# State decay product moved from GpSimd to ScalarE, and x added by an accumulating transfer

## What is computed

```
zxbcdt = xn @ in_proj_w.T            # z, x-B-C and dt per token
xBC    = silu(causal conv of 4 taps)
theta  = clip(theta_base + tanh(xn @ w1) @ w2, -pi/2, pi/2)
log_z  = complex(-(lambda + eta * theta**2) * dt, theta * dt)
# per chunk, with the running sum of log_z and the state of the chunk before:
S = exp(cumlog) * state + sum over s <= t of exp(cumlog_t - cumlog_s) B_s x_s
y = Re(C . S);  y = y + x_ssm * D
g = y * silu(z);  g = g * rsqrt(mean(g*g) + eps) * norm_w
mixer = g @ out_proj_w.T
expert = gate * (xn @ expert_w[idx] + expert_b[idx])
out = x + mixer + expert
```

## Time and profile before

| What | Value |
|---|---|
| median of three runs | 1242.69 us (1236.13 to 1245.13) |
| the profiled execution | 1231.05 us, its span 1229.2 us |
| TensorE matmul busy | 1063.8 us, 87% |
| VectorE busy | 1044.4 us, 85% |
| ScalarE busy | 815.0 us, 66% |
| GpSimd busy | 270.0 us, 22% |
| granted TensorE clock, mean | 0.942 |

### The profile page before, as it was taken

The page is one execution under the profiler, slowest core; times in us unless marked ns, Lnnn a source line. Parts: engine busy times, 40 slices in busy tenths (PEclk is TensorE's granted clock), DMA queues, the critical chain, the costliest instruction groups (busy, mean ns, idle before and its releaser), DMA issues.

```text
span 1229.2 us, 26224 instructions
## 1 busy us (share of the span) xinstructions
PE 1063.8 (87%) x8826; PEld 826.3 (67%) x8827; DVE 1044.4 (85%) x1934; ACT 815.0 (66%) x1453; POOL 270.0 (22%) x307
## 2 busy tenths in 40 slices
PE   3772299846899999999999999999999999999895
PEld 2441266544677777777777777777877777777674
DVE  5757923227999999999999999999999999999962
ACT  2441211108988888887888888888888888887650
POOL 1212676600011111221111111111122111111111
PEclk9895599977899999999999999999999999999997
DMA  6993155641444444444444444444444444444341
GB/s 231 360 363 122 35 163 178 168 119 45 146 145 149 144 153 143 148 136 150 152 148 144 144 151 152 144 153 144 144 136 146 154 145 150 145 148 144 125 138 33
DMA packets 144270, 185.55 MB, mean 151 GB/s; under 512 B 20142, under 2 KB 101343, under 8 KB 143760
## 3 DMA queue, kind: packets, MB, share of 16 engines
q1 hardware_dynamic: 122736, 146.70, 35.3%
q0 software_dynamic: 6528, 17.83, 5.6%
q10 hardware_dynamic: 14880, 19.40, 4.5%
HBM read 75.99 MB, written 40.63 MB: 95 GB/s over the span
## 4 chain that ended last, share of the span: by engine, by line
DVE 51%; issue 21%; PE 2%; POOL 1%; ACT 1%; DVEq 1%; DMA 0%; POOLq 0%; ACTq 0%
DVE conv L1143 13%; DVE att L1229 4%; DVE g L1247 3%; DVE prod L1202 3%; DVE decay L1176 3%; DVE prod L1201 3%; DVE prod L1212 3%; DVE prod L1211 3%; DVE o_tile L1269 2%; DVE phase L1168 2%; DVE x_tile L1254 2%; DVE lam L1160 2%; DVE state L1237 2%; DVE cown L1216 2%; DVE theta L1151 1%
## 5 line engine op out<-in xcount | busy, mean ns | idle before, releaser
L817 PE MATMUL ps<-xn_in,win 128*128 128x256 f32 x1152 | 289.5, 393 | 25.9 <-DMA xn_in<-xnT_d 15.6
L817 PEld LDWEIGHTS ps<-xn_in,win 128*128 128x128 f32 x1152 | 214.3, 195 | 57.3 <-issue 13.6
L1143 DVE SCALAR_TENSOR_TENSOR conv<-x_pre,col,conv 128x256 f32<-128x256 f32 x480 | 195.2, 479 | 15.6 <-ACT conv L984 15.5
L942 PE MATMUL ps<-wout,g 128*128 128x256 f32 x512 | 129.5, 398 | 23.8 <-DVE o_tile L1269 23.8
L1309 POOL TENSOR_TENSOR state_in<-state,cin_s 128x256 f32<-128x256 f32 x56 | 43.4, 775 | 478.3 <-DVE state L1237 478.3
L942 PEld LDWEIGHTS ps<-wout,g 128*128 128x128 f32 x512 | 97.9, 197 | 43.2 <-issue 29.4
L1322 POOL TENSOR_TENSOR rms<-ms,cst 128x1 f32<-128x1 f32 x64 | 46.6, 729 | 245.4 <-DVE ms L1261 245.4
L631 DVE TENSOR_TENSOR r_tiles<-ps,r_expw 128x256 f32<-128x256 f32 x72 | 30.6, 425 | 79.9 <-issue 73.7
L929 PEld LDWEIGHTS ps<-att,x_tok 128*64 128x64 f32 x1024 | 54.6, 136 | 49.6 <-issue 26.5
L984 ACT ACTIVATE conv<-ps,col 128x256 f32<-128x256 f32 x160 | 83.7, 572 | 0.0
L1229 DVE TENSOR_TENSOR att<-ps,cst 128x1024 f32<-128x1024 f32 x64 | 77.2, 1207 | 5.6 <-PE ps L902 5.6
(11 more groups left out here) (169 smaller groups left out, 2338.2 us busy)
## 6 DMA issues: line engine op xcount, KB each, us to landing
cin_s<-cin SPq DMA_DIRECT2D x128, 129.0 KB, 2.2
rep<-bc_d SPq DMA_DIRECT2D x128, 128.0 KB, 2.8
grow_s<-grow SPq DMA_DIRECT2D x128, 128.0 KB, 2.1
bup_s<-bup SPq DMA_DIRECT2D x128, 128.0 KB, 2.0
cown_s<-cown SPq DMA_DIRECT2D x128, 128.0 KB, 2.0
expert_d<-r_tiles ACTq DMA_DIRECT2D x18, 512.0 KB, 3.0
xn_d<-r_tokens SPq DMA_DIRECT2D x16, 512.0 KB, 9.1
xnT_d<-r_tiles ACTq DMA_DIRECT2D x16, 512.0 KB, 7.4
```

Of the source, the lines that this page charges most:

```text
L817: last = nc.tensor.matmul(dst, win[:, kt, n * P:(n + 1) * P], xn_in[b][:, kt, :], start=(kt == 0), stop=(kt == KT - 1))
L942: nc.tensor.matmul(bank_o[:, 0:D_MODEL], g[ch][:, q, :], wout[:, q, :], start=(q == 0), stop=(q == PAIRS - 1))
L1143: nc.vector.scalar_tensor_tensor(conv[:, ct, :], x_pre[b][:, ct, tap:tap + MT], c("conv_w", ct * D_CONV + tap), conv[:, ct, :], ALU.mult, ...
```

## The change

Four things are done together.

1. VectorE's `back_plus` is gone. The gathered expert rows land in `plus_tile` (two buffers per tile instead of one each of x and expert rows); ScalarE's new `back_scale` multiplies them by the gate in place; GpSimd's new `back_add_x` issues a transfer of x that adds into the same tile as it lands. SP's `load_x` is gone. `back_final` waits for that transfer and adds `plus_tile`.
2. The state's decay product moves from GpSimd (one instruction over 256 columns) to ScalarE (four of 64 columns, since ScalarE takes one scale per row).
3. The gather is issued one macro tile earlier.
4. The lists of steps of all five engines are written in another order.

```diff
@@ gpsimd_mixer
-                def back_state(m, ch):
-                    ...
-                    nc.gpsimd.tensor_tensor(state_in[1 - ch][:, :, :], state[:, :, :], by.broadcast_to([P, PAIRS, HEADDIM]), ALU.mult).then_inc(s["statein"], 1)
-
-                @macro
                 def back_gather(m, ch):
                     t = m * TPM + ch
-                    after(pool, s["xplus"], TPM * (m - 1) + ch + 1)
-                    pool.indirect_dma_start(e_tile[ch][:, :], None, expert_d, ...).then_inc(e_loaded2[ch], 16)
+                    after(pool, s["final"], t - 2 * TPM + 1)
+                    pool.indirect_dma_start(plus_tile[m % 2][ch][:, :], None, expert_d, ...).then_inc(e_loaded2[ch], 16)
+
+                @macro
+                def back_add_x(m, ch):
+                    t = m * TPM + ch
+                    pool.wait_ge(s["xplus"], t + 1)
+                    pool.dma_start(plus_tile[m % 2][ch][:, :], x[t * P:(t + 1) * P, :], accum_op=ALU.add).then_inc(x_loaded[ch], 16)
@@ scalar_mixer
+                def back_scale(m, ch):
+                    t = m * TPM + ch
+                    act.wait_ge(e_loaded2[ch], 16 * (m + 1))
+                    tile = plus_tile[m % 2][ch]
+                    nc.scalar.activation(tile[:, :], tile[:, :], ACT.Copy, scale=gate[:, t:t + 1]).then_inc(s["xplus"], 1)
+
+                @macro
+                def back_state(m, ch):
+                    b, t = m % 2, m * TPM + ch
+                    last = m % MPS == MPS - 1 and ch == TPM - 1
+                    act.wait_ge(s["stated"], t + 1)
+                    after(act, s["yout"], t)
+                    act.wait_ge(cin_landed[b], STACK * (m // 2 + 1))
+                    for n in range(PAIRS):
+                        by = zero_dec[:, n:n + 1] if last else cin_s[b][:, n, MT + ch:MT + ch + 1]
+                        done = nc.scalar.activation(state_in[1 - ch][:, n, :], state[:, n, :], ACT.Copy, scale=by)
+                    done.then_inc(s["statein"], 1)
@@ vector_mixer
-                def back_plus(m, ch):
-                    ...
-                    nc.vector.scalar_tensor_tensor(x_tile[ch][:, :], e_tile[ch][:, :], gate[:, t:t + 1], x_tile[ch][:, :], ALU.mult, ALU.add).then_inc(s["xplus"], 1)
@@ vector_mixer, the new list
+                    front_conv(m + 2, range(10, 15))
+                    back_mask(m, 0)
                     front_waves(m + 1)
+                    back_state(m, 0)
+                    front_cin(m + 1)
                     front_lamdt(m + 2)
-                    ...
                     back_gate(m, 0)
+                    front_bup(m + 1)
+                    front_phase(m + 2)
+                    back_state(m, 1)
+                    front_cown(m + 1)
                     back_mask(m, 1)
                     front_decay(m + 2)
                     back_ms(m, 0)
+                    front_clip(m + 3)
                     front_frac(m + 2)
                     back_final(m, 0)
+                    back_gate(m, 1)
                     front_conv(m + 3, range(0, 10))
                     back_ms(m, 1)
-                    ...
                     back_final(m, 1)
@@ gpsimd_mixer, the new list
+                    back_gather(m + 1, 0)
+                    back_gather(m + 1, 1)
                     back_rms(m, 0)
+                    back_add_x(m + 1, 0)
+                    back_add_x(m + 1, 1)
                     back_rms(m, 1)
```

More of the change, by code:

```diff
@@ L684, in whole_mixer @@
             zero_dec = wb("zero_dec", [P, PAIRS])
-            x_tile, e_tile, o_tile = ([wb(f"{n}{b}", [P, D_MODEL]) for b in range(2)] for n in ("x_tile", "e_tile", "o_tile"))
+            o_tile = [wb(f"o_tile{b}", [P, D_MODEL]) for b in range(2)]
+            plus_tile = [[wb(f"plus_tile{b}{ch}", [P, D_MODEL]) for ch in range(TPM)] for b in range(2)]
             ms, rms = ([wb(f"{n}{b}", [P, 1]) for b in range(2)] for n in ("ms", "rms"))
@@ L784, in load_x @@
                 @macro
-                def load_x(m):
-                    for ch in range(TPM):
-                        t = m * TPM + ch
-                        after(sp, s["final"], t - TPM + 1)
-                        sp.dma_start(x_tile[ch][:, :], x[t * P:(t + 1) * P, :]).then_inc(x_loaded[ch], 16)
-                @macro
                 def store(m, ch):
@@ L1249, in back_plus @@
                 @macro
-                def back_plus(m, ch):
-                    t = m * TPM + ch
-                    dve.wait_ge(x_loaded[ch], 16 * (m + 1))
-                    dve.wait_ge(e_loaded2[ch], 16 * (m + 1))
-                    nc.vector.scalar_tensor_tensor(x_tile[ch][:, :], e_tile[ch][:, :], gate[:, t:t + 1], x_tile[ch][:, :], ALU.mult, ALU.add).then_inc(s["xplus"], 1)
-                @macro
                 def back_ms(m, ch):
@@ L1266, in back_final @@
                     dve.wait_ge(s["rmsd"], t + 1)
-                    dve.wait_ge(s["xplus"], t + 1)
+                    dve.wait_ge(x_loaded[ch], 16 * (m + 1))
                     after(dve, o_stored[ch], 16 * m)
-                    nc.vector.scalar_tensor_tensor(o_tile[ch][:, :], bank_o[:, 0:D_MODEL], rms[ch][:, :], x_tile[ch][:, :], ALU.mult, ALU.add).then_inc(s["final"], 1)
+                    nc.vector.scalar_tensor_tensor(o_tile[ch][:, :], bank_o[:, 0:D_MODEL], rms[ch][:, :], plus_tile[m % 2][ch][:, :], ALU.mult, ALU.add).then_inc(s["final"], 1)
                 nc.vector.memset(hidden[0][32:LORA + 1, :], 1.0).then_inc(m_ready, 1)
```

89 lines of the change are left out of this document (35 added, 54 removed).

## The result

| | kernel before | changed kernel |
|---|---|---|
| median of 15 runs each | 1241.75 us (1236.13 to 1247.53) | 1233.92 us (1227.58 to 1237.79) |
| the profiled execution | 1231.05 us, span 1229.2 | 1235.43 us, span 1232.6 |

The ratio of the runs is 0.9925, 95% interval 0.9907 to 0.9944. That is 9.3 us less (7.0 to 11.5); forecast were 13.4 us.

What follows compares the result with a forecast made beforehand. VectorE was taken to bound the 29 mixer passes: -0.80 - 0.31 + 0.75 a pass gives -10.4 us, filling and draining -3, so 1242.69 - 13.4 = 1229 us. Its own range was 1221 to 1237, the wider one 1219 to 1250.

Steps and rivals of the forecast that it cites:

- VectorE's pace: In the 29 full mixer passes VectorE goes from 28.39 to 28.03 us a pass, 10.4 us in all.
- Additions gone: back_plus's two additions leave VectorE, 0.40 us of the engine each, 0.80 us less a pass.
- Scans relieved: VectorE's two phase scans take 1.31 instead of 1.62 us without GpSimd's product beside them, 0.31 us a pass gained.
- New wait: VectorE stands still for GpSimd's power between the second tile's back_ms and back_final, costing 0.75 us a pass.
- SP loses two loads of x per pass and issues nothing new ... The landing has a whole pass: The adding transfer replaces SP's loads of x and has a whole pass to land; no cost was counted for it.
- The start: Filling of the mixer nearly unchanged: conv behind clip, phase later, one ScalarE table load saved; -1 us.
- -3 for both ends: Filling at -1 and draining at -2 us together, with +3 and -7 as ends of the pair.
- The closest call: TensorE waits 0.6 us (0 to 1.1) for xn_in's load, median 4.1; its pace 28.0 against VectorE's 28.03.
- The rival with a chance of 0.2: The xn_in load sets the pace: at 4.6 us landing the passes gain nothing, time stays at 1243; chance 0.2.
- TensorE's own work: TensorE's work in a full mixer pass without its wait for o_tile, taken as about 27.4 us.
- ScalarE and GpSimd: off the path: ScalarE at 25.8 us a pass (24.8 to 27.2) fits under 28.03; GpSimd's adding issues, about 1 us each, stay hidden.
- the rival at 3.1 us: Adding-transfer issues hold GpSimd's second power beyond 3.1 us each, making the kernel slower, 1281 us at 4.0; chance 0.06.

Runs made afterwards that it cites:

- j_plus_and_product: Kernel before in its own order, with VectorE's two additions replaced and the state product on ScalarE; ratio 0.9729 to the kernel before, passes of 27.20 us.
- e_add_first: Changed kernel with GpSimd's two adding transfers moved to the start of the pass that uses them, ahead of the gathers; ratio 0.9892 to the kernel before.
- b_no_adding: Changed kernel without the two adding transfers of x, x missing from the output, back_final waiting for ScalarE's scaling; ratio 0.9950 to the kernel before.
- i_plus_alone: Kernel before in its own order, only VectorE's two additions replaced by scaling and adding transfer, state product left on GpSimd; ratio 0.9823, passes of 27.53 us.
- h_final_late_add_first: Changed kernel with second tile's back_final behind five convolution steps and adding transfers at the start of the pass using them; ratio 0.9724 to the kernel before.
- a_cin_early: Changed kernel with SP's copy of cin issued ahead of the copy of bup instead of last; ratio 1.0147 to the kernel before.

## Why the forecast was right, and by how much not

**VectorE's pace: right, each term.** The kernels take the sum apart. Additions gone: -0.80 forecast, 28.32 to 27.53, -0.79. Scans relieved: -0.31, 27.53 to 27.20, -0.33. New wait: +0.75, 27.20 to 27.96 between j_plus_and_product and the new order, and back to 27.20 when only the wait is covered, 0.76 both times. The undisturbed pass lost 0.36 us, as forecast. (28.03 stood in the forecast because I started from the mean of 28.39. That mean holds two disturbed passes of the kernel before, 29.32 and 29.34 us, together 2.0 us too long. In each of them the granted clock falls, to 0.57 at the mean from 855 to 859 and from 1111 to 1115 us. The undisturbed pass is 28.32.)

**The step that failed in size: "SP loses two loads of x per pass and issues nothing new ... The landing has a whole pass".** I asked when the adding transfer must have landed, and never what it does to the transfers beside it. It stands beside the copy of `cin`, which the new order had put last on SP, with little time before its readers. Five passes after the first are 0.6 to 1.1 us too long, 4.1 us in all. Moving the adding transfers away takes all five out (e_add_first), which is 4.1 us by the ratios too, though the two intervals just overlap.

**The start: -1 forecast, a loss of about 3 in place of it.** The first full pass begins with the mask that the old order had done in its own time ahead. VectorE waits for TensorE's scores there (the idle time is in the middle stretch above). TensorE, then VectorE:

```profile
337.26 2.08 PE L891 MATMUL ps<-cown_s,grow_s 64*128 64x128 f32 x16 [3.50 <-DMA cin_s<-cin]
339.27 1.12 PE L895 MATMUL ps<-cin_s,bup_s 64*64 64x64 f32 x16
```

```profile
340.53 1.23 DVE L1245 TENSOR_TENSOR att<-ps,cst 128x1024 f32<-128x1024 f32 x1 [2.54 <-PE ps L895]
```

TensorE waits 3.50 us for the copy of `cin` and then does the scores at a granted clock of 0.54 at the mean (334 to 341 us): 2.08 and 1.12 us, where they take 1.16 and 0.68 at the full clock. In e_add_first VectorE's wait is 2.51 us and the first pass 28.82, against 28.85. That doesn't clear the neighbours, though. In that one pass e_add_first has its adding transfers and gathers (319.88 to 324.73) beside the copy (321.29 to 323.96) as well, and the copy lands in 3.7 to 3.9 us. In b_no_adding only the gathers stand there, the copy lands in 2.0 to 4.0 us, and VectorE waits 2.66. So the adding transfer isn't what makes this wait; how much of it the gathers do stays open. With it the account closes: 29 x 27.96 = 810.8 us, 2.5 for this wait, 0.9 for the rest of the first pass, 4.1 for the five long ones, together 818.3, against 818.52. The forecast's -3 for both ends is the measured -1.7, before these 3.4 are added. The kernel before took 29 x 28.32 + 2.0 = 823.3, so of the 10.5 us that the undisturbed passes gained, 4.8 are left in the middle stretch.

**The closest call was not close.** `xn_in` lands in 3.2 us, not 4.1, and TensorE doesn't wait. Its issue had stood beside a gather (in the kernel before at 751.16, the second gather at 751.10); in i_plus_alone both stand at 750.74, and the load takes 4.2 us; in the changed kernel it is issued 3.5 us after the second gather's start, and in j_plus_and_product 2.0 us after the first one's: 3.2 and 3.3. In j_plus_and_product, and in e_add_first too (3.2), a second gather's issue does begin within 0.7 us of the load's, but there it is held for 6.33 and 3.61 us, and the gathers land in 8.3 and 4.7 us at the median against 2.8 in the changed kernel; I take it that the load was through before they moved. The rival with a chance of 0.2 had been priced by a duration that belonged to the old neighbour. By this reading it was the same effect as with `cin`, in the other direction; no run of its own shows it. And 27.4 us for TensorE's own work was too much: h_final_late_add_first runs at 27.2. So both of TensorE's terms were too high, its own work and its wait of 0.6 us. Their sum had come to 0.03 us under VectorE's pace by chance; neither had a say, because VectorE set the pace.

**ScalarE and GpSimd: off the path, as forecast.** ScalarE is busy 24.7 us a pass against 25.8 (24.8 to 27.2), just under the lower end. Product and scaling last what was taken, 0.34 and 0.51 us, but the sum took them at their durations, and neighbours on ScalarE overlap: the four products take 0.96 us from the first one's start to the next instruction's (854.76 to 855.72), not 4 x 0.32. Issues of 1.1 us against "about 1"; the rival at 3.1 us was far off.

## What to carry to other kernels

Test the parts of a bundled change in the old order before adopting a new one: here the two replacements were worth 2.7%, and the order that came with them gave back nearly three quarters of it, most of it in one wait that five instructions could have covered. A landing time read from a trace belongs to the neighbours that the transfer had there: when an order moves a transfer to or from the moment of another queue's transfers, take the other value, and ask which reader then has no slack. A queue whose copies take 2.5 us each to issue is a line in which every step moved forward moves another one back. And before pricing a new wait of TensorE by its length, look at the granted clock behind it: in a_cin_early the late copy cost 0.1 us in a pass without a fall of the clock and 2.3 us in one with it.

## What the runs showed that I had not expected

- GpSimd and VectorE hold each other up, in both directions: GpSimd's product lasts 0.62 us beside VectorE's mask (one input in PSUM), 1.06 beside its scans, 2.66 beside two of its products from SBUF.
- GpSimd's issue of a gather is held too. Beside VectorE's products it lasted 6.33 us in j_plus_and_product against 1.0 us in the changed kernel, and 3.61 in e_add_first:

```profile
743.94 6.33 POOL L1313 DMA_INDIRECT plus_tile<-expert_d,slot_of  x1 [0.80 <-DVE o_tile L1279]
```

  It hurt neither kernel, since each gather has a whole pass. That VectorE's products are the cause is argued from their being there (743.58 to 750.65, two inputs in SBUF throughout), not shown by a run of its own. Two inputs in SBUF alone aren't enough: in the changed kernel both gathers' issues stand beside VectorE's convolution steps, which read two SBUF tiles each, and last 1.09 and 1.00 us. Nor does the held issue end with VectorE's stretch, but 0.38 us before it, at 750.27.
- SP's copy of `cin` lands in 2.1 us at the median (3.9 to 4.3 at most) without a transfer of x from GpSimd's queue beside it, and in 3.0 (5.5 to 5.6 at most) with one of 128 KB per tile, adding or plain. The load of `xn_in` lands in 3.2 against 4.2, with a gather as the likely neighbour.
- TensorE's granted clock can fall right behind a wait for a copy, to 0.57 at the mean over the next 4 us, but doesn't each time: it did behind 13 of the 26 waits for `bup` in a_cin_early. What decides it these runs don't show.
- GpSimd's power after a bare wait for another semaphore starts 0.16 us later than after an issue. This stays open.
